# The depthwise convolutions of a fused attention and GRU kernel on GpSimd: eight time steps at a time in place of two

## What is computed

```python
x = x + _L0_cond_ref(x, cond_2048[:, None, :], ...)        # attention
x = x + _L1_cond_ref(cond_2048, x, W_ih, W_hh, b_ih, b_hh)  # GRU: 512 steps, one after the other
x = x + _L2_cond_ref(x, cond_2048[:, None, :])              # conv, 4 taps, w = cond
x = x + _L3_cond_ref(x, cond_2048[:, None, :], L3_cond_b)   # conv, the same taps, + bias

def cell(h, x):
    gi = x @ W_ih + b_ih
    gh = h @ W_hh + b_hh
    r = sigmoid(i_r + h_r); z = sigmoid(i_z + h_z)
    n = tanh(i_n + r * h_n)
    h_new = (1.0 - z) * n + z * h
```

## Time and profile before

| | |
|---|---|
| median of three runs | 2158.68 us (2157.4 to 2159.33) |
| profiled execution | 2154.03 us, its span 2152.2 us |
| granted TensorE clock | 0.997 of full |
| PE, PEld busy | 2087.6, 1574.0 us (97%, 73%) |
| DVE, ACT, POOL busy | 1386.3, 1174.6, 1122.1 us (64%, 55%, 52%) |
| instructions on POOL | 3876 |

### The profile page before, as it was taken

The page is one execution under the profiler, slowest core; times in us unless marked ns, Lnnn a source line. Parts: engine busy times, 40 slices in busy tenths (PEclk is TensorE's granted clock), DMA queues, the critical chain, the costliest instruction groups (busy, mean ns, idle before and its releaser), DMA issues.

```text
span 2152.2 us, 183070 instructions
## 1 busy us (share of the span) xinstructions
PE 2087.6 (97%) x76192; PEld 1574.0 (73%) x76192; DVE 1386.3 (64%) x5140; ACT 1174.6 (55%) x5995; POOL 1122.1 (52%) x3876
## 2 busy tenths in 40 slices
PE   8999999999999999999999999999999999999998
PEld 2222222222389999999999999999999999998887
DVE  4344444344367777777777777777777777777776
ACT  3444444443255555555555555555555555555555
POOL 0243323323146666666666666666666666666665
PEclk9999999999999999999999999999999999999999
DMA  6000000001122212221222221222121212210001
GB/s 255 1 1 1 1 1 1 1 21 60 38 68 52 54 48 54 52 54 51 69 56 54 52 53 49 55 59 65 49 57 48 58 47 60 65 30 10 5 7 19
DMA packets 218062, 95.89 MB, mean 45 GB/s; under 512 B 170216, under 2 KB 213480, under 8 KB 217320
## 3 DMA queue, kind: packets, MB, share of 16 engines
q1 hardware_dynamic: 217032, 92.00, 16.4%
q10 hardware_dynamic: 928, 2.65, 0.3%
HBM read 26.30 MB, written 12.58 MB: 18 GB/s over the span
## 4 chain that ended last, share of the span: by engine, by line
PE 63%; DVE 8%; issue 1%; DMA 0%; SPq 0%; ACT 0%; DVEq 0%
PE ps L1199 57%; DVE arena L1024 5%; PE ps L1227 4%; PE ps L1238 2%; DVE arena L1030 1%; DVE arena L1036 1%; DVE arena L1041 1%; DMA arena<-arena 0%; DVE arena L1108 0%; DVE arena L1111 0%; SPq L952 0%; DVE arena L1114 0%; ACT ps L1132 0%; DVE arena L1117 0%; DVE seq L1054 0%
## 5 line engine op out<-in xcount | busy, mean ns | idle before, releaser
L1199 PE MATMUL ps<-whh,arena 128*4 128x128 f32 (+1 forms) x65536 | 1447.7, 246 | 36.4 <-DVE arena L1041 33.0
L1199 PEld LDWEIGHTS ps<-whh,arena 128*4 128x4 f32 x65536 | 1299.9, 87 | 142.4 <-DVE arena L1041 64.4
L1024 DVE STREAM_TRANSPOSE arena<-ps 128x128 f32<-128x128 f32 x1024 | 436.3, 426 | 226.3 <-PE ps L1199 226.2
L1157 ACT ACTIVATE arena<-arena 128x8 f32<-128x8 f32 x1024 | 215.9, 211 | 637.1 <-DVE arena L1024 637.0
L1271 POOL TENSOR_TENSOR arena<-tap,seq 128x32 f32<-128x32 f32 x1020 | 230.6, 258 | 217.7 <-DVE seq L1054 217.7
L437 DVE TENSOR_REDUCE top<-ps 128x2 f32<-128x1024 f32 x128 | 150.8, 1220 | 253.7 <-PE ps L693 253.6
L1041 DVE TENSOR_TENSOR_SCAN arena<-arena 128x24 f32<-128x24 f32 x1024 | 213.7, 209 | 145.1 <-ACT arena L1168 145.1
L1132 ACT ACTIVATE ps<-arena 128x128 f32<-128x128 f32 x1026 | 269.6, 263 | 0.4 <-PEq L207 0.4
L1271 POOL TENSOR_TENSOR arena<-tap,arena 128x32 f32<-128x32 f32 x1020 | 231.0, 257 | 66.5 <-POOL arena L1281 66.5
L1030 DVE STREAM_TRANSPOSE arena<-ps 128x64 f32<-128x64 f32 x1024 | 257.8, 252 | 12.1 <-PE ps L1199 1.7
L268 POOL TENSOR_TENSOR arena<-arena 128x2048 f32<-128x2048 f32 x16 | 72.8, 4548 | 344.3 <-ACT arena L343 344.3
(11 more groups left out here) (96 smaller groups left out, 1385.2 us busy)
## 6 DMA issues: line engine op xcount, KB each, us to landing
arena<-arena SPq DMA_DIRECT2D x216, 114.0 KB, 2.2
arena<-arena SPq DMA_DIRECT2D x112, 128.0 KB
arena<-seq SPq DMA_DIRECT2D x224, 55.0 KB
arena<-gi_d SPq DMA_DIRECT2D x248, 32.0 KB
gi_d<-arena SPq DMA_DIRECT2D x96, 57.0 KB, 2.3
out<-seq SPq DMA_DIRECT2D x14, 256.0 KB
seq<-in_x SPq DMA_DIRECT2D x3, 1024.0 KB, 15.2
whh<-in_w_hh SPq DMA_DIRECT2D x1, 3072.0 KB, 22.5
```

The source lines that it names most:

```text
L1024: e.transpose(trn[:, h].rearrange("p q (i c s) -> p q c i s", c=2, s=2)[:, :, :, :, 0], bank[RN[h]][:, 0:P].rearrange("p (q c i) -> p q c ...
L1157: e.activation(r_d0[:, h].rearrange("p (i s) -> p i s", s=2)[:, :, 1], trn[:, h, 0, 0:2 * NH].rearrange("p (i s) -> p i s", s=2)[:, :, 0], ...
L1199: last = e.matmul(bank[dst[h]][32 * G:32 * G + B, 0:n], hv, wv[:, k, gates, G, 64 * h:64 * h + 64], start=False, stop=k2 == 1 and k == C - ...
```

## The change

GpSimd's loop takes eight steps at a time (NB = 8) and has 13 operations for them in place of 60. Each is four times as wide: a product has 16 x 8 = 128 elements. The four products lie in four parts of `prd`; `conv_halves` adds two pairs of them in one operation of 256 elements, and one more addition of 128 sums the rest. The addition of the input to its convolution is folded into the last tap, which is the condition plus one. `tap` and `b3x` lose their last dimension and are broadcast along the eight steps. The waits for `s_pool` stay, seven in an iteration.

The second part is `let_in(m)`: the iteration doesn't run through once its first eight steps are there, but waits at eight places for `s_x3` at it * 8 + 8 + m, m = 0 to 7, that is for the addition L1054 of one of the next eight steps. Between them stand: two products (m = 0), two (1), the halves (2), the sum into `seq2` and the first product on `seq2` (3), two products (4), one (5), the halves (6), the sum and, behind its own wait, the addition of the bias into `seq` (7). In slots 2, 3, 6 and 7 the wait for `s_x3` is followed by one for `s_pool`.

VectorE computes the last eight steps' convolutions at the end, with the same 13 operations.

```diff
@@ -88,8 +88,8 @@
         sT = sb("sT", [P, 2, C, 32])
         gqs = sb("gqs", [P, 1])
         eps = sb("eps", [P, 1])
-        tap = sb("tap", [P, TAPS, NI, 2])
-        b3x = sb("b3x", [P, NI, 2])
+        tap = sb("tap", [P, TAPS, NI])
+        b3x = sb("b3x", [P, NI])
         seq_cb = seq[:].rearrange("p (c b) t -> p c b t", c=C)
         s_apart = sem("s_apart")
@@ -169,7 +169,7 @@
         r_d0 = tile([P, 2, 2 * NH])
         pre = tile([P, 2, 2 * NH])
         z_d0 = tile([P, 2, HS])
-        prd = tile([P, 2, TAPS * NI * 2])
+        prd = tile([P, 8 * NI * 2 * TAPS])
         st = {n: sem(n) for n in ("s_clear", "s_open", "s_h", "s_rn", "s_z", "s_tr", "s_sig", "s_pre",
                                   "s_tanh", "s_seed_rn", "s_seed_z", "s_x3", "s_pool", "s_rzpart", "s_ataken", "s_npart", "s_nfree",
                                   "s_nseed", "s_npair")}
@@ -520,11 +520,12 @@
                 for c in range(C):
                     d = wout[:, c, P * c:P * c + P]
                     e.tensor_tensor(d, d, ident[:], ALU.add).then_inc(d_wout, 1)
-                for s in range(2):
-                    for c in range(C):
-                        e.tensor_copy(tap[:, :, B * c:B * c + B, s], vecT[:, c, 0:TAPS].rearrange("p (k a) -> p k a", a=1)
-                                      .broadcast_to([P, TAPS, B]))
-                        e.tensor_copy(b3x[:, B * c:B * c + B, s], vecT[:, c, R_B3:R_B3 + 1].broadcast_to([P, B]))
+                for c in range(C):
+                    items = slice(B * c, B * c + B)
+                    e.tensor_copy(tap[:, 0:PAD, items], vecT[:, c, 0:PAD].rearrange("p (k a) -> p k a", a=1).broadcast_to([P, PAD, B]))
+                    e.tensor_scalar(tap[:, PAD, items], vecT[:, c, PAD:TAPS].broadcast_to([P, B]), 1.0, None, ALU.add)
+                    e.tensor_copy(b3x[:, items], vecT[:, c, R_B3:R_B3 + 1].broadcast_to([P, B]))
                 for n in range(NS):
                     if n + 1 < NS:
                         maxima(n + 1, 0)
@@ -924,8 +925,25 @@
         n_fixed = tile([P, 2, P])
         n_moving = tile([P, 2, CW])
-        POOL_OPS, END_OPS = 9, 5 + 2 * TAPS
+        NB, POOL_OPS, END_OPS = 8, 7, 13
+        wide = NB * NI
         s_store, s_end = sem("out_store"), sem("s_end")
+        def conv_part(i):
+            return prd[:, wide * i:wide * i + wide].rearrange("p (i s) -> p i s", s=NB)
+        def along(v):
+            return v.rearrange("p (i s) -> p i s", s=1).broadcast_to([P, NI, NB])
+        def conv_product(e, src, k, t):
+            return e.tensor_tensor(conv_part(k), along(tap[:, k]), src[:, :, bass.ds(t + k, NB)], ALU.mult)
+        def conv_halves(e):
+            return e.tensor_tensor(prd[:, 4 * wide:6 * wide], prd[:, 0:2 * wide], prd[:, 2 * wide:4 * wide], ALU.add)
         stores = [(P * i, P, 4 * j, 4) for i in range(TB - 1) for j in range(4)]
@@ -933,7 +951,7 @@
         def store(e, first, n, item, items):
             if first + n < T:
-                e.wait_ge(st["s_pool"], POOL_OPS * ((first + n) // 2))
+                e.wait_ge(st["s_pool"], POOL_OPS * ((first + n) // NB))
             else:
                 e.wait_ge(s_end, END_OPS)
             e.dma_start(out[:, item:item + items, first:first + n], seq[:, item:item + items, first:first + n]).then_inc(s_store, 16)
@@ -1097,28 +1115,24 @@
                         step(it * 2 + v, v)
-                t, done = T - 2, s_end
-                products = prd[:, 0].rearrange("p (k i s) -> p k i s", k=TAPS, s=2)
-                total = prd[:, 1, 0:2 * NI].rearrange("p (i s) -> p i s", s=2)
-                e.wait_ge(st["s_pool"], POOL_OPS * (T // 2 - 1))
+                t, done = T - NB, s_end
+                e.wait_ge(st["s_pool"], POOL_OPS * (T // NB - 1))
                 e.wait_ge(st["s_x3"], T)
-                n = 0
-                for src in (seq, seq2):
-                    for k in range(TAPS):
-                        e.tensor_tensor(products[:, k], tap[:, k], src[:, :, t + k:t + k + 2], ALU.mult).then_inc(done, 1)
-                    n += TAPS
-                    e.wait_ge(done, n)
-                    e.tensor_reduce(total, prd[:, 0].rearrange("p (k w) -> p w k", k=TAPS), AX.X, ALU.add).then_inc(done, 1)
-                    e.wait_ge(done, n + 1)
-                    if src is seq:
-                        e.tensor_tensor(seq2[:, :, t + PAD:T + PAD], seq[:, :, t + PAD:T + PAD], total, ALU.add).then_inc(done, 1)
-                        n += 2
-                    else:
-                        e.tensor_tensor(total, total, b3x[:], ALU.add).then_inc(done, 1)
-                        e.wait_ge(done, n + 2)
-                        e.tensor_tensor(seq[:, :, t:T], seq2[:, :, t + PAD:T + PAD], total, ALU.add).then_inc(done, 1)
-                        n += 3
-                    e.wait_ge(done, n)
+                for k in range(TAPS):
+                    conv_product(e, seq, k, t).then_inc(done, 1)
+                e.wait_ge(done, 4)
+                conv_halves(e).then_inc(done, 1)
+                e.wait_ge(done, 5)
+                e.tensor_tensor(seq2[:, :, t + PAD:T + PAD], conv_part(4), conv_part(5), ALU.add).then_inc(done, 1)
+                e.wait_ge(done, 6)
+                for k in range(TAPS):
+                    conv_product(e, seq2, k, t).then_inc(done, 1)
+                e.wait_ge(done, 10)
+                conv_halves(e).then_inc(done, 1)
+                e.wait_ge(done, 11)
+                e.tensor_tensor(conv_part(6), conv_part(4), conv_part(5), ALU.add).then_inc(done, 1)
+                e.wait_ge(done, 12)
+                e.tensor_tensor(seq[:, :, t:T], conv_part(6), along(b3x[:]), ALU.add).then_inc(done, 1)
             @block.scalar
             def _(e):
@@ -1250,45 +1264,50 @@
                 with e.Fori(2 * BODIES, T // 2) as it:
                     for v in range(2):
                         step(it * 2 + v, v)
             @block.gpsimd
             def _(e):
                 e.wait_ge(st["s_clear"], N_CLEAR)
                 s = st["s_pool"]
                 def wait(sem_, n):
                     e.wait_ge(sem_, n)
                     e.sem_inc(s_apart, 1)
-                with e.Fori(0, T // 2 - 1) as it:
-                    t = e.snap(it * 2)
-                    t3 = e.snap(it * 2 + PAD)
-                    wait(st["s_x3"], it * 2 + 2)
-                    def conv(src, n):
-                        for k in range(TAPS):
-                            w = 2 * NI
-                            last = e.tensor_tensor(prd[:, 0, w * k:w * k + w].rearrange("p (i s) -> p i s", s=2),
-                                                   tap[:, k], src[:, :, bass.ds(t + k, 2)], ALU.mult)
-                        last.then_inc(s, 1)
-                        wait(s, it * POOL_OPS + n)
-                        e.tensor_tensor(prd[:, 1, 0:64], prd[:, 0, 0:64], prd[:, 0, 64:128], ALU.add).then_inc(s, 1)
-                        wait(s, it * POOL_OPS + n + 1)
-                        e.tensor_tensor(prd[:, 1, 64:96], prd[:, 1, 0:32], prd[:, 1, 32:64], ALU.add).then_inc(s, 1)
-                        wait(s, it * POOL_OPS + n + 2)
-                    part = prd[:, 1, 64:96].rearrange("p (i s) -> p i s", s=2)
-                    conv(seq, 1)
-                    e.tensor_tensor(seq2[:, :, bass.ds(t3, 2)], seq[:, :, bass.ds(t3, 2)], part, ALU.add).then_inc(s, 1)
+                with e.Fori(0, T // NB - 1) as it:
+                    t = e.snap(it * NB)
+                    def let_in(m):
+                        wait(st["s_x3"], it * NB + NB + m)
+                    let_in(0)
+                    conv_product(e, seq, 0, t)
+                    conv_product(e, seq, 1, t)
+                    let_in(1)
+                    conv_product(e, seq, 2, t)
+                    conv_product(e, seq, 3, t).then_inc(s, 1)
+                    let_in(2)
+                    wait(s, it * POOL_OPS + 1)
+                    conv_halves(e).then_inc(s, 1)
+                    let_in(3)
+                    wait(s, it * POOL_OPS + 2)
+                    e.tensor_tensor(seq2[:, :, bass.ds(it * NB + PAD, NB)], conv_part(4), conv_part(5), ALU.add).then_inc(s, 1)
+                    wait(s, it * POOL_OPS + 3)
+                    conv_product(e, seq2, 0, t)
+                    let_in(4)
+                    conv_product(e, seq2, 1, t)
+                    conv_product(e, seq2, 2, t)
+                    let_in(5)
+                    conv_product(e, seq2, 3, t).then_inc(s, 1)
+                    let_in(6)
                     wait(s, it * POOL_OPS + 4)
-                    conv(seq2, 5)
-                    e.tensor_tensor(prd[:, 1, 96:128].rearrange("p (i s) -> p i s", s=2), part, b3x[:], ALU.add).then_inc(s, 1)
-                    wait(s, it * POOL_OPS + 8)
-                    e.tensor_tensor(seq[:, :, bass.ds(t, 2)], seq2[:, :, bass.ds(t3, 2)],
-                                    prd[:, 1, 96:128].rearrange("p (i s) -> p i s", s=2), ALU.add).then_inc(s, 1)
```

(8 more changed lines are left out.)

## The result

The changed kernel takes 2170.61 us (median of six runs, 2169.96 to 2171.71), the kernel before beside it 2159.01 us (2156.63 to 2161.27): a ratio of 1.0061, with an interval from 1.0051 to 1.0070, or 13 us; the two medians lie 11.6 us apart. It is slower, as forecast, and inside the range; the forecast said 19 us.

What follows compares the result with a forecast made beforehand. Bound: the recurrent loop of TensorE products, VectorE scans and ScalarE, with GpSimd counting only through delays. Terms 10.4 + 7.4 + 1.1 - 1.0 + 1.2 = +19.1 us gave 2173.1 profiled, 2177.8 us as median; range 2158 to 2187.

Steps and rivals of the forecast that it cites:

- Little to gain in the loop: Recurrence loop: removing today's stalls of VectorE's scans by GpSimd saves only 1.0 us, all there is to gain there.
- The port: VectorE two-SBUF-input operations starting 0.03 us after a GpSimd operation's start to 0.14 us before its end are held until then.
- Starts: GpSimd starts after L1054: slot 3 at 0.64 and 1.36 us, slot 7 at 0.56 and 1.28, with second wait 0.17.
- Slot 3: Product on seq2 holds the scan at 1.41 us by 0.27 us in half of 55 iterations: +7.4 us.
- Slot 7: Second addition holds the scan at 1.41 us by 0.19 us in all 55 unrolled iterations: +10.4 us.
- The end: Last eight steps' convolutions on VectorE after the last step, with wider operations, all exposed: +1.2 us.
- The last 64 steps: Scan at 1.32 us is ahead of slot 3, level with slot 7; held 0.28 us in half of eight: +1.1 us.
- the forecast case: Unrolled steps: slot 7 held and slot 3 partly, +12 to +22 us; chance 0.39.
- the rival of a cheap second wait: GpSimd's second wait costs less than 0.17 us, shrinking both stalls; at zero cost +9.2 us, 2168; chance 0.15.
- The rival without collisions: GpSimd 0.10 us later than thought, scans come first in both slots; only -1.0 + 1.2 remains, 2159 us; chance 0.15.
- that with both slots held: Slots 3 and 7 both collide fully, GpSimd starting a little earlier: +27.7 us, 2186; chance 0.25 for over +22.
- The rival that GpSimd costs every step something unseen: Scans are held today as later starts, 0.02 us per step over 512 steps: -10.2 us, 2149.7; chance 0.06.

## Why the prediction was right, and where its sizes were off

- *What bounds the kernel*, and that GpSimd's share counts only through the scans: right. Halving GpSimd's work gained nothing, and with none of it the time was the same (1.0002).
- *Little to gain in the loop* (-1.0 us): right in size. With as many instructions on VectorE as before the last 64 steps took 193.6 us against 193.7 before, slot 7's stalls of 1.0 us among them, so the stalls removed were worth some 1.1, by single profiles.
- *The port, its release 0.14 us before the end and the first to start having it*: right, in slot 3 of the changed kernel (0.38 us), in the copy (0.15) and in the start that 0.02 us decided. One of the rows behind the rule doesn't fit its words: L448 is a `TENSOR_SCALAR` with one tensor input, so for operations with two inputs the 0.14 us rested on L1036 alone.
- *Starts*: the sum 0.61 us after the addition, reckoned 0.64; the product 1.33, reckoned 1.36; L1307 0.53, reckoned 0.56. The second wait of 0.17 was 0.15.
- *Slot 3*: "held in half of the iterations" was the mis-sized term in one way: it was held in all 55, as the product started 0.02 us earlier than reckoned and my margin of 0.02 us was nearer 0.05. In the other way each stall was 0.19 us in place of 0.27, because of that earlier start and because a product with a broadcast input takes 415 ns, not 456 (L942 beside L1294, 458). Reckoned 7.4 us, measured 55 x 0.188 = 10.3; moving the product gave back 9.5 (a product of slot 4 moved with it).
- *Slot 7*: 0.025 us in place of 0.19. The bias addition starts 0.19 us behind the one before it, not 0.26: I had charged it an address step that the row of L1309 doesn't show, and the operation itself takes 408 ns. Reckoned 10.4, measured 55 x 0.025 = 1.4 us. This is the term that was sized wrong, and it makes up more than the forecast's excess.
- *The end*, +1.2: right, 7.7 against 6.5 us. *The last 64 steps*: slot 7 was held in each of the eight iterations by about 0.13 us, 1.0 in all, where I had half of them at 0.28, 1.1. That these steps came out 1.1 us longer and not level goes with the four instructions fewer on VectorE, of which the sum had nothing.

That the total came so near is in part luck. Slot 7 was 9.0 us too large, slot 3 2.9 too small, and 1.0 us in the last 64 steps was missing: 19.1 - 9.0 + 2.9 + 1.0 = 14.0, where the traces have 13.7. The picture was the other way round, too: it had slot 7 held always and slot 3 in half of the iterations, and slot 3 was held always and slot 7 hardly. So the scan of 0.38 us stood beside slot 3's product and not beside slot 7's addition, which started 1.17 us after the addition of the state and not 1.28; the scans' mean was 205 ns and not 212, and GpSimd's busy share 25% and not 27.

The measured 11.6 to 13.7 us lie at the lower edge of the forecast case (+12 to +22), beside the rival of a cheap second wait (+5 to +12). That rival's reason was not the one: the wait cost 0.15 us. The rival without collisions came true only in the kernel in which the two places were mended, at 2157 us; that with both slots held named the right slots, but slot 7's stall was an eighth of what it had. The rival that GpSimd costs every step something unseen falls with the idle GpSimd, 2159.64 us.

## What to carry to other kernels

Beside a latency-bound loop the work of a second engine is worth its moments, not its busy time: 60 short operations cost about 1 us in all, 13 wide ones 11 us more in the unrolled steps, and moving two of them by a slot gave back 9.5. Where VectorE's two-input operations are on the path, lay GpSimd's reading operations so that each ends before, or begins after, their start, measured from the event that lets them in; count the sequencer's waits and address steps for that, and place waits that are already fulfilled ahead of the one that gates. Before such a change, take the neighbour's work out altogether once: here that would have shown that there was next to nothing to win.

## What the runs showed of the hardware

- A GpSimd operation that only writes (memset, 0.69 us) doesn't hold a VectorE scan that starts inside it; one with a single input (copy, 0.61 us) does.
- Who starts first has the port, within a few hundredths of a us: a scan 0.02 us ahead of the product was not held and the product lengthened by 0.02, a scan 0.08 us behind it was held for 0.19. In the run without pacing 42 additions of the state that began up to 0.01 us behind a GpSimd addition were not held.
- GpSimd adds or multiplies 128 elements in 415 or 408 ns where one input is broadcast along the inner dimension, and in 458 where none is.
- A fulfilled wait (with its raise of `s_apart`) behind a gating one costs GpSimd 0.15 us; an additional one between two operations 0.10.
- Four more instructions in VectorE's set-up made a loop far behind them faster by 0.03 us in every second step.
- The attention stage ended at either 596 to 597 or 599 to 600 us in profiled executions of kernels that share it or nearly so: 3 us which a comparison of two single profiles would put down to a change.
